# An attention and expert kernel on one core: router squares and sums reordered on ScalarE, seven masked expert inputs instead of eight, the drain's last steps in another order

## The chip, the cores and the metric

The kernel runs on one core of a Trainium2 chip. The metric is the device time of one execution in microseconds (us). Shown are three runs of the kernel before and one execution taken by the hardware profiler.

## The reference

`x` has 16 images of 256 positions and 128 channels. For each image the reference computes

```
h = layernorm(x) * (1 + ca) + sa
x = x + ga * attn(h)
h = layernorm(x) * (1 + cb) + sb
x = x + gb * ffn(h)
```

with the six modulation vectors from `silu(c) @ wmod`. `attn` computes from `h` a frequency and a phase for each position, interpolates `h` at 33 sampling points around the position, weighs them by a kernel computed from `h` (8 heads), and ends with `silu(out @ out_w.T)`. `ffn` is what the change touches:

```
logits = h @ router_w.T + router_b
_, top_k_indices = top_k(softmax(logits), 2)
mask = one_hot(top_k_indices, 8).sum(axis=-2)
out = einsum('bse,ehd,bsd->bsh', mask, expert_w, h) + einsum('bse,eh->bsh', mask, expert_b)
```

Each position has two experts, so its eight mask values sum to 2.

## The kernel before, in words

The work is cut into nine units (`UNITS`): one image, seven pairs, one image. `LAST` is unit 8, `LATE` unit 7. Each engine has its own program, written out by hand in order; semaphores tie them together. There is no scheduler: the order on an engine is the order of the calls in its loop. Loop `i` on each engine takes work of several units: the front of unit `i+1` (and its statistics of unit `i+2`), the middle of unit `i`, the back of units `i-1` and `i-2`. A call `run(i, lag, stage)` does `stage` for unit `i+lag` if there is one; `second` does it only for pairs.

- **VectorE (DVE).** The resampling matrix of an image is made in `T` by a network of six predicated copies (`network`, L802), then multiplied by the hat weights `c` into `AT`: `spread_out`, L835, four products for a pair, two for each image, each followed by `set_ends` (L845). Between the products of the two images stand small steps: `places` (L758, `eI`), `moves` (L763), `logits` (L868), `stage_masks` (L773), `best` (L874, L877), `offset` (L780, `sf`), `hits` (L884). `cells_from` (L789, `near`) follows the second pair of products. `masked` (L902) multiplies the transposed second input `h2T` by the eight expert masks, 8 x 256 elements an image. `residual` (L854) adds the attention's output, in the PSUM bank `pY`, to `x` and sums it; `total` (L907) adds the experts' output. `line` (L723 to L735) makes `nlf` from ScalarE's `th`, `product` (L813) the two small products.
- **ScalarE (ACT).** It copies and scales what TensorE leaves in PSUM: `mid_A` (L507), `mid_ao` (L515), `mid_y` (L522), `mid_gate` (L529), `back_h2T` (L540), `back_mk` (L549), `back_moe` (L556). The row statistics are its too: `sums1` (L382), `squares1` and `stats2` (L368 for the mean, L371 for the squares), `norm1` and `norm2` (L405). `front_u` (L472, L479) needs `nlf`.
- **GpSimd (POOL).** For each statistic it makes `ve` (L321), the power `rs` (L327) and `nm` (L329), first `rstd2` of unit `i-1`, then `rstd1` of unit `i+2`. `norm1` and `norm2` wait for `nm`.
- **TensorE (PE).** `mid_A` (L1051) transposes `AT`, `mid_attend` (L1065) multiplies by the values, `mid_y` (L1075) by `out_w`, `mid_gate` (L1081) transposes back into `pY`. `back_x2T` (L1091), `back_logits` (L1102) and `back_mk` (L1112) belong to the router, `back_experts` (L1136, with the bias matmul L1153) to the experts, `back_out` (L1158) transposes the experts' output back. `warm_up` (L985) are matmuls whose result nobody reads.
- **SyncE's queue.** `masks` writes the mask rows to memory and loads them back, spread over the partitions (`mkb`). The last two units get their masks by TensorE instead (`back_mb`, L1124), in four quarters of two experts.

After the loops each engine has a drain, written out call by call, in which the units `LATE-1`, `LATE` and `LAST` end. There the output of the experts of `LATE` goes to `pY`, and the statistics of `LATE` and `LAST` are VectorE's (L706 to L715).

```
                run(i, 2, sums1)
                run(i, 1, front_u)
                run(i, -1, norm2)
...
                run(i, -1, back_h2T)
                run(i, -2, back_moe)
                run(i, 2, squares1)
                run(i, 0, mid_A, 0)
```

Of the kernel before, what the change touches and what calls it, by code (L numbers as in the profile page):

```python
# [86 lines left out]
def build(nc, t):  # L87

    ctx = ExitStack()
    with ctx:  # L90
# [32 lines left out]
        sel = sb("sel", [NP * E, E, P], BF16)  # L123
# [53 lines left out]
        d_out = sem("d_out")  # L177
# [7 lines left out]
        g_nm1 = sem("g_nm1"); g_nm2 = sem("g_nm2")  # L185
# [83 lines left out]
        def _(sp):  # L269
# [19 lines left out]
            def masks(n):  # L289
# [6 lines left out]
                sp.dma_start(scratch[n % 2][:, 0:w], mkT[0:E, 0:w]).then_inc(d_mk, 16)  # L296
# [3 lines left out]
                sp.dma_start(mkb[n % 2][:, :, 0:w], spread(scratch[n % 2][:, 0:w], [P, E, w], 0)).then_inc(d_mkb[n % 2], 16)  # L300
# [55 lines left out]
        def _(act):  # L356
# [263 lines left out]
        def _(dve):  # L620
# [295 lines left out]
            for i in range(-1, LAST):  # L916
# [12 lines left out]
                run(i, 0, network, range(5, 6))  # L929
                run(i, 1, line)  # L930
# [39 lines left out]
            total(LATE - 1)  # L970
# [8 lines left out]
        def _(pe):  # L979
# [136 lines left out]
            def back_mb(n, b):  # L1116
# [23 lines left out]
            def back_biases(n, b, dst):  # L1140
                if n < LATE:
                    pe.wait_ge(v_hm, before(n) + b + 1)
                if b == 0:
# [137 lines left out]
```

## Time and profile before

| what | value |
|---|---|
| three runs | 293.69, 294.6, 295.03 us; median 294.6 |
| the profiled execution's own time | 293.6 us |
| its span, first to last instruction | 291.8 us |
| busy VectorE | 262.0 us, 90% |
| busy TensorE (matmuls) | 262.0 us, 90% |
| busy ScalarE | 226.9 us, 78% |
| busy GpSimd | 62.7 us, 21% |
| mean granted TensorE clock | 0.998 |
| ScalarE's waits for GpSimd's `nm` | 16.1 us in 10 |

The profile is of one execution. The span leaves out some 1.8 us around the instructions. "Busy" is the share in which an engine executes; a busy TensorE includes the matmuls that only keep it going. Times in the rows further down are us from the start of the span.

### The profile page before, as it was taken

What the parts mean: (1) busy time and instruction counts of PE and PEld (TensorE: products, weight loads), DVE (VectorE), ACT (ScalarE), POOL (GpSimd) and SP (SyncE); (2) the same over time, 40 slices, a digit from 0 to 9 for tenths busy, and PEclk for the clock granted to TensorE, in tenths of its full rate; (3) what the DMA queues carried; (4) which work ended last, traced back from release to release, by engine and by line L of the source; (5) the groups of instructions that cost most, each with busy time, mean ns of one, the idle gap of its engine ahead of it and who ended that gap; (6) DMA issues with size and microseconds to landing.
All of it is one profiled execution on the core that took longest, in us unless ns stands there. A gap on an engine that the chain in (4) does not pass through costs nothing.

```text
span 291.8 us, 5429 instructions
## 1 busy us (share of the span) xinstructions
PE 262.0 (90%) x1867; PEld 181.0 (62%) x1876; DVE 262.0 (90%) x543; ACT 226.9 (78%) x641; POOL 62.7 (21%) x59
## 2 busy tenths in 40 slices
PE   8899886899798999889998999889999989899995
PEld 3544642665486487647784569548884768476664
DVE  7989989998979999999999899989999999982671
ACT  4885899699897998699869989799779767655310
POOL 4103101800451023502080026202340300010100
PEclk9999999999999999999999999999999999999999
DMA  6560000020004000320014000500041004100101
GB/s 179 161 160 0 0 0 0 3 74 1 1 2 163 2 1 0 97 86 3 0 29 155 0 0 2 183 2 1 2 130 53 1 0 125 60 2 0 36 2 54
DMA packets 12011, 12.93 MB, mean 44 GB/s; under 512 B 1021, under 2 KB 10960, under 8 KB 11216
## 3 DMA queue, kind: packets, MB, share of 16 engines
q1 hardware_dynamic: 11540, 12.19, 13.9%
q10 hardware_dynamic: 444, 0.40, 0.5%
q8 instruction: 15, 0.25, 0.3%
q14 instruction: 12, 0.10, 0.1%
HBM read 10.44 MB, written 2.15 MB: 43 GB/s over the span
## 4 chain that ended last, share of the span: by engine, by line
ACT 31%; PE 26%; DVE 18%; POOL 12%; issue 11%; ACTq 0%; DVEq 0%; POOLq 0%
PE pE L1136 9%; ACT A L507 8%; DVE AT L835 8%; POOL rs L327 8%; ACT xn L405 4%; ACT c L490 4%; POOL nm L329 4%; PE pE L985 3%; ACT xn L371 3%; DVE T L802 3%; PE pY L1136 3%; PE pR L1028 2%; ACT hT L428 2%; ACT y L529 2%; DVE hm L902 2%
## 5 line engine op out<-in xcount | busy, mean ns | idle before, releaser
L802 DVE COPY_PREDICATED T<-mask,T 128x1472 f32<-128x1472 int16 (+9 forms) x54 | 76.2, 1411 | 0.5
L835 DVE TENSOR_TENSOR AT<-T,c 128x2064 f32<-128x2064 f32 x32 | 72.3, 2300 | 0.0
L1136 PE MATMUL pE<-hm,late 128*128 128x256 f32 x224 | 52.6, 386 | 0.0
L1136 PEld LDWEIGHTS pE<-hm,late 128*128 128x128 f32 x224 | 41.2, 190 | 6.6
L507 ACT ACTIVATE A<-pT 128x512 f32<-128x512 f32 x64 | 34.7, 600 | 12.6 <-PE pT L1051 12.5
L327 POOL TENSOR_TENSOR rs<-ve,mhalf 128x4 f32<-128x4 f32 (+1 forms) x18 | 32.5, 1806 | 44.3 <-DVE ve L715 37.5
L321 POOL TENSOR_SCALAR ve<-sq 128x4 f32<-128x4 f32 (+1 forms) x14 | 7.0, 502 | 162.9 <-ACT xn L371 162.9
L405 ACT ACTIVATE xn<-x,nm,rs 128x128 f32<-128x128 f32 x64 | 26.5, 485 | 16.1 <-POOL nm L329 16.1
L1051 PE MATMUL pT<-first,AT 128*128 128x128 f32 x256 | 34.2, 276 | 4.8 <-DVE AT L845 4.7
L1051 PEld LDWEIGHTS pT<-first,AT 128*128 128x128 f32 x256 | 28.3, 141 | 11.4 <-DVE AT L845 9.9
L507 ACT ACTIVATE A<-pR 128x512 f32<-128x512 f32 x64 | 35.2, 619 | 0.0
L1065 PE MATMUL pY<-A,hs 128*32 128x256 f32 x512 | 33.3, 384 | 1.7 <-ACT A L507 1.4
L1051 PE MATMUL pR<-first,AT 128*128 128x128 f32 x256 | 33.6, 274 | 0.0
L902 DVE TENSOR_TENSOR hm<-mkb,h2T 128x2048 f32<-128x2048 bf16 x13 | 29.6, 2276 | 0.0
L1051 PEld LDWEIGHTS pR<-first,AT 128*128 128x128 f32 x256 | 28.7, 141 | 0.6
L490 ACT ACTIVATE c<-near,early 128x172 f32<-128x172 f32 (+1 forms) x54 | 26.2, 571 | 0.0
L1028 PE MATMUL pR<-proj,hT 128*128 128x297 f32 x62 | 23.8, 465 | 0.9 <-ACT hT L428 0.9
L1065 PEld LDWEIGHTS pY<-A,hs 128*32 128x32 f32 x512 | 16.7, 109 | 12.1 <-ACT A L507 7.4
L985 PE MATMUL pE<-warm 128*128 128x512 bf16 x85 | 22.1, 415 | 1.3 <-DVE warm L643 1.2
L329 POOL TENSOR_TENSOR nm<-mu,rs 128x4 f32<-128x4 f32 (+1 forms) x18 | 21.0, 1165 | 1.4
L371 ACT ACTIVATE xn<-x,mu 128x128 f32<-128x128 f32 x52 | 20.2, 390 | 0.5
L985 PEld LDWEIGHTS pE<-warm 128*128 128x128 bf16 x88 | 9.2, 107 | 12.0 <-issue 2.8
(145 smaller groups left out, 389.2 us busy)
## 6 DMA issues: line engine op xcount, KB each, us to landing
mkb<-mask_rows SPq DMA_DIRECT2D x6, 1024.0 KB, 5.3
x<-in_x SPq DMA_DIRECT2D x7, 256.0 KB, 6.1
out<-x SPq DMA_DIRECT2D x7, 256.0 KB, 5.3
late<-in_late SPq DMA_DIRECT2D x1, 592.0 KB, 3.9
mkb<-mask_rows SPq DMA_DIRECT2D x1, 512.0 KB, 3.6
x<-in_x SPq DMA_DIRECT2D x2, 128.0 KB, 3.7
wmod<-in_wmod ACTq DMA_DIRECT2D x1, 256.0 KB, 3.5
out<-x SPq DMA_DIRECT2D x2, 128.0 KB, 3.2
```

The source lines that it names most:

```text
L327: nc.gpsimd.tensor_tensor(rs[:, 0:w], ve[:, 0:w], mhalf[:, 0:w], ALU.pow).then_inc(out, 1)
L329: nc.gpsimd.tensor_tensor(nm[:, 0:w], mu[:, 0:w], rs[:, 0:w], ALU.mult).then_inc(last, 1)
L405: ins = nc.scalar.activation(xn[:, bt, :], of_x(n)[:, bt, :], ACT.Identity, bias=nm[:, bt:bt + 1], scale=rs[:, bt:bt + 1])
L490: nc.scalar.activation(cells[:, :, :, r], near[:, 0:w, :], ACT.Abs, bias=off[:, r:r + 1]).then_inc(a_abs, 1)
L507: nc.scalar.activation(A[b][:, m, 2 * j:2 * j + 2, :].rearrange("p h l -> p (h l)"), four_banks(k)[:, :], ACT.Copy).then_inc(a_A, 1)
L802: nc.vector.copy_predicated(rows[:, :, :, j0:j1], spread(mask[:, k, 0:w, j0:j1], [P, w, H, j1 - j0], 2), rows[:, :, :, j0 + (1 << bit):j1 ...
L835: nc.vector.tensor_tensor(cells_of(bt).rearrange("p h (j r) -> p h j r", r=BLK), spread(T[n % 2][:, bt, 0:H, 0:NB], [P, H, NB, BLK], 3), s ...
L902: nc.vector.tensor_tensor(hm[b][:, :, :], mkb[n % 2][:, :, b * L:(b + 1) * L], spread(own, [P, E, L], 1), ALU.mult).then_inc(v_hm, 1)
L985: mm(bank[:, :], warm[:, 0:P], warm[:, :], start=True, stop=True)
L1051: ins = nc.tensor.transpose(four_banks(k)[:, c0:c0 + P], AT[:, 2 * b + i, 2 * j + a, OVER + m * P:OVER + (m + 1) * P], ident)
L1065: ins = mm(pY[32 * j:32 * j + 32, b * L:(b + 1) * L], hs[n % 2][:, 2 * b + m, hh, :], A[b][:, m, hh, :], start=(m == 0 and a == 0), stop=( ...
L1136: ins = mm(dst, weT[:, e, :], hm[b][:, e, :], start=False, stop=(e == E - 1))
```

## The change

The change has three parts.

1. *Experts.* Since the eight mask values of a position sum to 2, the sum over eight masked experts is written as `2 W7 h` plus the sum over seven of `mask_e (W_e - W7) h`. `expert_weights` makes the differences and the doubled `W7` once, in loop 1 (`selectors` moves from loop 0's end to behind its network). `masked` then makes seven inputs, the mask transfers and `back_mb` carry seven, and `back_plain` multiplies `h2T` by `2 W7`, 512 columns for a pair, with one bias matmul for both images.
2. *Order in the loops.* On ScalarE `sums1` goes behind `norm2`, and `squares1` ahead of `back_moe`. On TensorE the last two experts of a pair go behind `back_x2T`, and four warm-ups of each loop from 3 on go. In loop `LATE` the masks of unit `LATE-1` are made between the two halves of `mid_A`, and their transfer is issued by image.
3. *The drain.* On VectorE both masked products of `LATE-1`, `residual(LATE)` and `stats2(LATE)` come ahead of the last `AT` product, which also waits for `rs2`. ScalarE and TensorE follow that order.

```diff
             def masks(n):
...
-                sp.dma_start(scratch[n % 2][:, 0:w], mkT[0:E, 0:w]).then_inc(d_mk, 16)
+                sp.dma_start(scratch[n % 2][:, 0:w], mkT[0:EM, 0:w]).then_inc(d_mk, 16)
...
+                parts = ((0, L, d_mkb[n % 2]), (L, w, d_mkl)) if n == LATE - 1 else ((0, w, d_mkb[n % 2]),)
+                for c0, c1, landed in parts:
+                    sp.dma_start(mkb[n % 2][:, :, c0:c1],
+                                 spread(scratch[n % 2][:, c0:c1], [P, EM, c1 - c0], 0)).then_inc(landed, 16)
...
# ScalarE, loop
-                run(i, 2, sums1)
                 run(i, 1, front_u)
                 run(i, -1, norm2)
                 if i < 0:
                     run(i, 1, front_hs)
+                run(i, 2, sums1)
                 run(i, -1, back_h2T)
+                run(i, 2, squares1)
                 run(i, -2, back_moe)
-                run(i, 2, squares1)
-                run(i, 0, mid_A, 0)
-                run(i, -1, back_mk)
+                run(i, 0, mid_A, 0, (0,))
+                if i == LATE:
+                    back_mk(LATE - 1)
+                run(i, 0, mid_A, 0, (1,))
+                if i < LATE:
+                    run(i, -1, back_mk)
                 run(i, 2, norm1)
...
# ScalarE, drain
             mid_gate(LATE)
+            back_moe(LATE - 1)
+            norm2(LATE)
+            back_h2T(LATE)
             mid_A(LAST, 0)
-            norm2(LATE)
+            back_mk(LATE)
             mid_ao(LAST)
-            back_h2T(LATE)
             mid_y(LAST)
             mid_gate(LAST)
-            back_mk(LATE)
-            back_moe(LATE - 1)
             norm2(LAST)
...
# VectorE
+            def expert_weights():
+                dve.wait_ge(d_late, 32)
+                nc.vector.tensor_tensor(weT[:, 0:EM, :], weT[:, 0:EM, :], spread(weT[:, EM, :], [P, EM, C], 1),
+                                        ALU.subtract).then_inc(v_we, 1)
+                dve.wait_ge(v_we, 1)
+                nc.vector.tensor_scalar(weT[:, EM, :], weT[:, EM, :], 2.0, None, ALU.mult).then_inc(v_we, 1)
...
                 run(i, 0, network, range(5, 6))
+                if i == 0:
+                    selectors()
+                elif i == 1:
+                    expert_weights()
                 run(i, 1, line)
...
-            network(LAST, range(2, 6))
+            network(LAST, range(2, 3))
             masked(LATE - 1, 0)
+            network(LAST, range(3, 5))
+            masked(LATE - 1, 1)
+            network(LAST, range(5, 6))
+            residual(LATE)
+            stats2(LATE)
+            dve.wait_ge(g_rs2, LATE + 1)
             spread_out(LAST, 0)
             spread_out(LAST, 1)
             set_ends(LAST, 0)
-            masked(LATE - 1, 1)
-            residual(LATE)
-            stats2(LATE)
             route(LATE)
             residual(LAST)
             stats2(LAST)
+            total(LATE - 1)
             masked(LATE, 0)
-            total(LATE - 1)
...
# TensorE
+            def back_plain(n):
...
+                w = tiles(n) * P
+                mm(moe_bank(n)[:, 0:w], weT[:, EM, :], h2T_of(n)[:, 0:w], start=True, stop=False)
+                mm(moe_bank(n)[:, 0:w], ebp[:, :], mkT_of(n)[:, 0:w], start=False, stop=False)
...
                 run(i, -2, back_experts, 0)
-                second(i, -2, back_experts, 1)
+                second(i, -2, back_experts, 1, range(0, 5))
                 if i == 1:
-                    warm_up(18)
+                    warm_up(23)
...
                 run(i, -1, back_x2T)
-                if i > 0:
+                second(i, -2, back_experts, 1, range(5, EM))
+                if 0 < i < 3:
                     warm_up(4, pT[0])
...
+            back_experts(LATE - 1, 0, range(0, 4))
             mid_y(LATE)
-            back_experts(LATE - 1, 0)
+            back_experts(LATE - 1, 0, range(4, EM))
             mid_gate(LATE)
+            back_experts(LATE - 1, 1)
+            warm_up(6, pT[0])
+            back_x2T(LATE)
+            back_out(LATE - 1)
+            back_logits(LATE)
+            warm_up(4, pT[0])
             mid_A(LAST, 0, 0)
             mid_A(LAST, 0, 1)
+            back_mk(LATE)
             mid_attend(LAST, 0, 0)
             mid_attend(LAST, 0, 1)
...
```

How the instructions stand now, at the three places that matter. ScalarE, in a steady loop, from the squares of the second statistic to the first copy of `A`. Before:

```order
L368 ACTIVATE mu2<-sum2 128x4
L371 ACTIVATE xn2,sq2<-x,mu2 128x128 x4
L452 ACTIVATE hs1<-pX 128x16x2x16
L382 ACTIVATE xn1,sum1<-x 128x128 x4
L472 ACTIVATE u<-early,nlf,invf 128x50 x4
L479 ACTIVATE uR<-u 128x200
L405 ACTIVATE xn2<-x,nm2,rs2 128x128 x4
L540 ACTIVATE h2T<-pX,modT 128x256 x2
L556 ACTIVATE moeT<-pE,modT 128x256 x2
L368 ACTIVATE mu1<-sum1 128x4
L371 ACTIVATE xn1,sq1<-x,mu1 128x128 x4
L507 ACTIVATE A0<-pT0 128x512
```

Now:

```order
L373 ACTIVATE mu2<-sum2 128x4
L376 ACTIVATE xn2,sq2<-x,mu2 128x128 x4
L457 ACTIVATE hs1<-pX 128x16x2x16
L477 ACTIVATE u<-early,nlf,invf 128x50 x4
L484 ACTIVATE uR<-u 128x200
L410 ACTIVATE xn2<-x,nm2,rs2 128x128 x4
L387 ACTIVATE xn1,sum1<-x 128x128 x4
L545 ACTIVATE h2T<-pX,modT 128x256 x2
L373 ACTIVATE mu1<-sum1 128x4
L376 ACTIVATE xn1,sq1<-x,mu1 128x128 x4
L561 ACTIVATE moeT<-pE,modT 128x256 x2
L512 ACTIVATE A0<-pT0 128x512
```

The sums (`xn1,sum1`) moved behind `norm2` (`xn2<-x,nm2,rs2`), the router squares (`mu1`, `xn1,sq1`) ahead of `moeT`.

VectorE, in the drain, from the last network's third stage on; `T0` is the matrix of `LAST`, `hm0` and `hm1` are the masked inputs of the two images of `LATE-1`. Before:

```order
L802 COPY_PREDICATED T0<-mask,T0 128x2x8x46 x2
L802 COPY_PREDICATED T0<-mask,T0 128x2x8x44
L802 COPY_PREDICATED T0<-mask,T0 128x2x8x43
L902 TENSOR_TENSOR hm0<-mkb0,h2T 128x2048
L835 TENSOR_TENSOR AT<-T0,c 128x8x258 x2
L845 COPY AT<-endw 128x16x2
L902 TENSOR_TENSOR hm1<-mkb0,h2T 128x2048
L854 SCALAR_TENSOR_TENSOR x,sum2<-pY,x 128x128 x4
L706 BN_STATS st2<-x 128x6 x4
L710 BN_AGGR mv2<-st2 128x2 x4
L714 TENSOR_SCALAR mu2<-mv2 128x4
L715 TENSOR_SCALAR ve2<-mv2 128x4
```

Now:

```order
L923 TENSOR_TENSOR hm1<-mkb0,h2T 128x1792
L820 COPY_PREDICATED T0<-mask,T0 128x2x8x43
L872 SCALAR_TENSOR_TENSOR x,sum2<-pY,x 128x128 x4
L724 BN_STATS st2<-x 128x6 x4
L728 BN_AGGR mv2<-st2 128x2 x4
L732 TENSOR_SCALAR mu2<-mv2 128x4
L733 TENSOR_SCALAR ve2<-mv2 128x4
L853 TENSOR_TENSOR AT<-T0,c 128x8x258 x2
L863 COPY AT<-endw 128x16x2
L886 TENSOR_TENSOR lg<-pL,rb 128x32
```

The last `AT` product moved from ahead of the second masked product to behind the statistics of `LATE`.

TensorE, in the drain, around `mid_y(LATE)` (L1075, `pY<-aoT`). Before:

```order
L1065 MATMUL pY<-A1,hs1 32x256 x16
L1075 MATMUL pY<-aoT,late 128x512
L1153 MATMUL pE<-mkT,ebp 128x256
L1136 MATMUL pE<-hm0,late 128x256 x8
L1081 MATMUL pY<-first,y 128x128 x4
```

Now:

```order
L1094 MATMUL pY<-A1,hs1 32x256 x16
L1185 MATMUL pE<-h2T,late 128x512
L1186 MATMUL pE<-mkT,ebp 128x512
L1167 MATMUL pE<-hm0,late 128x256 x4
L1104 MATMUL pY<-aoT,late 128x512
L1167 MATMUL pE<-hm0,late 128x256 x3
L1110 MATMUL pY<-first,y 128x128 x4
L1167 MATMUL pE<-hm1,late 128x256 x7
L1014 MATMUL pT0<-warm 128x512 x6
L1120 MATMUL pX<-first,xn2 128x128 x4
```

The plain matmul (`pE<-h2T`), the bias and four experts of `LATE-1` moved ahead of `mid_y`.

## Rows read from the trace of the kernel before

**Rows 1.** Busy time by stretch: length; PE, PEld, DVE, ACT, POOL busy; clock; DMA

```profile
127.55:159.33 31.78, 29.18 (x218) 21.01 (x218) 30.46 (x57) 28.17 (x84) 8.48 (x6) 1.00 0.15 43
```

**Rows 2.** Timeline of VectorE, 140 to 174 (start us, length us, engine, line, operation)

```profile
139.29 4.52 DVE L835 TENSOR_TENSOR AT<-T,c 128x2064 f32<-128x2064 f32 x2
...
146.02 0.32 DVE L780 SCALAR_TENSOR_TENSOR sf<-sc,u 128x172 f32<-128x172 f32 x1
...
146.53 4.52 DVE L835 TENSOR_TENSOR AT<-T,c 128x2064 f32<-128x2064 f32 x2
...
163.44 0.29 DVE L854 SCALAR_TENSOR_TENSOR x<-pY,x 128x128 f32<-128x128 f32 x1 [0.99 <-PE pY L1081]
...
168.82 0.16 DVE L734 SCALAR_TENSOR_TENSOR nlf<-lp,invf 128x4 f32<-128x4 f32 x1
...
171.06 4.52 DVE L835 TENSOR_TENSOR AT<-T,c 128x2064 f32<-128x2064 f32 x2
```

**Rows 3.** Timeline of ScalarE (ACT), 140 to 174

```profile
142.23 1.02 ACT L540 ACTIVATE h2T<-pX,modT 128x256 f32<-128x256 f32 x2 [0.75 <-PE pX L1091]
...
143.85 0.21 ACT L368 ACTIVATE mu<-sum 128x4 f32<-128x4 f32 x1
...
152.59 1.65 ACT L405 ACTIVATE xn<-x,nm,rs 128x128 f32<-128x128 f32 x4 [2.54 <-POOL nm L329]
...
166.52 0.19 ACT L368 ACTIVATE mu<-sum 128x4 f32<-128x4 f32 x1
...
168.77 0.29 ACT L382 ACTIVATE xn<-x 128x128 f32<-128x128 f32 x1
...
169.94 1.37 ACT L472 ACTIVATE u<-early,nlf,invf 128x50 f32<-128x50 f32 x4
...
171.62 1.63 ACT L405 ACTIVATE xn<-x,nm,rs 128x128 f32<-128x128 f32 x4
```

**Rows 4.** Timeline of GpSimd (POOL), 140 to 174

```profile
146.19 6.00 POOL L327 TENSOR_TENSOR rs<-ve,mhalf 128x4 f32<-128x4 f32 x1
...
170.03 0.77 POOL L329 TENSOR_TENSOR nm<-mu,rs 128x4 f32<-128x4 f32 x1
```

**Rows 5.** Timeline of GpSimd, round 2

```profile
83.36 1.01 POOL L327 TENSOR_TENSOR rs<-ve,mhalf 128x4 f32<-128x4 f32 x1
...
84.44 4.47 POOL L329 TENSOR_TENSOR nm<-mu,rs 128x4 f32<-128x4 f32 x1
```

**Rows 6.** Groups by line and form, the masked product

```profile
L902 DVE TENSOR_TENSOR hm<-mkb,h2T 128x2048 f32<-128x2048 bf16 x13 | 29.6, 2276 | 0.0
```

**Rows 7.** Timeline of TensorE (PE), 140 to 174

```profile
160.00 1.12 PE L1075 MATMUL pY<-aoT,late 128*128 128x512 f32 x2
...
165.83 3.72 PE L1136 MATMUL pE<-hm,late 128*128 128x256 f32 x16
```

**Rows 8.** Timeline of VectorE, rounds 1 and 2

```profile
43.52 0.22 DVE L723 TENSOR_REDUCE sums<-th 128x8 f32<-128x64 f32 x1 [0.96 <-ACT th L463]
...
81.93 0.19 DVE L868 TENSOR_TENSOR lg<-pL,rb 128x32 f32<-128x32 f32 x1 [1.92 <-PE pL L1102]
```

**Rows 9.** Timeline of TensorE, the drain

```profile
250.91 1.12 PE L1075 MATMUL pY<-aoT,late 128*128 128x512 f32 x2 [0.94 <-ACT aoT L515]
...
260.70 2.26 PE L1065 MATMUL pY<-A,hs 128*32 128x256 f32 x32
...
272.46 0.28 PE L1153 MATMUL pY<-mkT,ebp 24*128 24x256 bf16 x1
```

**Rows 10.** Timeline of VectorE, the drain

```profile
256.81 0.20 DVE L845 COPY AT<-endw 128x32 f32<-128x32 f32 x1
...
259.10 0.29 DVE L854 SCALAR_TENSOR_TENSOR x<-pY,x 128x128 f32<-128x128 f32 x1
...
269.17 0.28 DVE L854 SCALAR_TENSOR_TENSOR x<-pY,x 128x128 f32<-128x128 f32 x1
```

**Rows 11.** Timeline of GpSimd, the drain

```profile
261.77 1.01 POOL L327 TENSOR_TENSOR rs<-ve,mhalf 128x4 f32<-128x4 f32 x1 [29.68 <-DVE ve L715]
```

More of the change, by code:

```diff
@@ L20 @@
 E = 8
+EM = E - 1
 EPS = 1e-5
@@ L159, in build @@
         mkT = sb("mkT", [NP * E, BT * P], BF16); mkL = sb("mkL", [NP * E, L], BF16)
-        mkb = [sb(f"mkb{i}", [P, E, BT * P], BF16) for i in range(2)]
-        hm = [sb(f"hm{i}", [P, E, L]) for i in range(2)]
+        mkb = [sb(f"mkb{i}", [P, EM, BT * P], BF16) for i in range(2)]
+        hm = [sb(f"hm{i}", [P, EM, L]) for i in range(2)]
         moeT = sb("moeT", [P, BT * P])
-        scratch = nc.dram_tensor("mask_rows", (2, E, BT * P), BF16, kind="Internal").ap()
+        scratch = nc.dram_tensor("mask_rows", (2, EM, BT * P), BF16, kind="Internal").ap()
         pT = [bank("pT0"), bank("pT1")]
@@ L901, in masked @@
                     dve.wait_ge(d_mkb[n % 2], 16 * (n // 2 + 1))
+                elif n == LATE - 1:
+                    dve.wait_ge(d_mkl, 16)
                 nc.vector.tensor_tensor(hm[b][:, :, :], mkb[n % 2][:, :, b * L:(b + 1) * L],
-                                        spread(own, [P, E, L], 1), ALU.mult).then_inc(v_hm, 1)
+                                        spread(own, [P, EM, L], 1), ALU.mult).then_inc(v_hm, 1)
             def total(n):
@@ L1122, in back_mb @@
                         pe.wait_ge(v_hm, masked_before(before(n) + b - 1) + k + 1)
-                    for a in range(2):
+                    for a in range(min(2, EM - 2 * k)):
                         ins = mm(four_banks(k)[:, a * L:(a + 1) * L], sel[:, 2 * k + a, :], mkT_of(n)[:, b * L:(b + 1) * L],
@@ L1126, in back_mb, with back_experts @@
                     ins.then_inc(t_mb, 1)
-            def back_experts(n, b, own=range(E)):
+            def back_experts(n, b, own=range(EM)):
                 img = before(n) + b
-                dst = moe_bank(n)[:, b * L:(b + 1) * L]
                 if own[0] == 0:
-                    back_biases(n, b, dst)
+                    if b == 0:
+                        back_plain(n)
+                    if n < LATE:
+                        pe.wait_ge(v_hm, img + 1)
                 for e in own:
@@ L1135, in back_experts @@
                         pe.wait_ge(v_hm, masked_before(img) + e // 2 + 1)
-                    ins = mm(dst, weT[:, e, :], hm[b][:, e, :], start=False, stop=(e == E - 1))
-                if own[-1] == E - 1:
+                    ins = mm(moe_bank(n)[:, b * L:(b + 1) * L], weT[:, e, :], hm[b][:, e, :], start=False,
+                             stop=(e == EM - 1 and b == UNITS[n][1] - 1))
+                if own[-1] == EM - 1:
                     ins.then_inc(t_moe, 1)
[L1140 to L1143, printed above, removed]
-                    pe.wait_ge(a_mk, n + 1)
-                    if n == 0:
-                        pe.wait_ge(v_ebp, 8)
-                    if n == LATE:
-                        pe.wait_ge(v_x2, NU)
-                    elif n == LAST:
-                        pe.wait_ge(v_out, LATE)
-                    elif n > 0:
-                        pe.wait_ge(v_out, n)
-                mm(dst, ebp[:, :], mkT_of(n)[:, b * L:(b + 1) * L], start=True, stop=False)
+            def back_plain(n):
+                if n == 0:
+                    pe.wait_ge(v_ebp, 8)
+                    pe.wait_ge(v_we, 2)
+                if n == LATE:
+                    pe.wait_ge(v_x2, NU)
+                elif n == LAST:
+                    pe.wait_ge(v_out, LATE)
+                elif n > 0:
+                    pe.wait_ge(v_out, n)
+                pe.wait_ge(a_mk, n + 1)
+                w = tiles(n) * P
+                mm(moe_bank(n)[:, 0:w], weT[:, EM, :], h2T_of(n)[:, 0:w], start=True, stop=False)
+                mm(moe_bank(n)[:, 0:w], ebp[:, :], mkT_of(n)[:, 0:w], start=False, stop=False)
             def back_out(n):
@@ L1194, in _ @@
                 run(i, -2, back_out)
+                if i == LATE:
+                    back_mk(LATE - 1)
                 run(i, 0, mid_A, 0, 1)
-                run(i, -1, back_mk)
+                if i < LATE:
+                    run(i, -1, back_mk)
                 run(i, 0, mid_attend, 0, 0)
@@ L1224, in _ @@
             back_mb(LATE, 1)
-            back_experts(LATE, 0, range(6, E))
+            back_experts(LATE, 0, range(6, EM))
             back_experts(LATE, 1, range(0, 3))
@@ L1229, in _ @@
             back_mb(LAST, 0)
-            back_experts(LATE, 1, range(6, E))
+            back_experts(LATE, 1, range(6, EM))
             back_experts(LAST, 0, range(0, 4))
             back_out(LATE)
-            back_experts(LAST, 0, range(4, E))
+            back_experts(LAST, 0, range(4, EM))
             back_out(LAST)
```

26 lines of the change are left out of this document (9 added, 17 removed).

## The prediction

> **What bounds the kernel now.** I read the busy shares of a steady round first. A round is the work between the first `AT` product of one unit and that of the next; round i is the one of loop i. VectorE is busy 30.46 of 31.78 us, TensorE 29.18, ScalarE 28.17, at a granted clock of 1.00 [rows 1]. The product starts at 139.29 and again at 171.06, so a round takes 31.77. VectorE idles once worth mention: 0.99 us ahead of `residual`, for `pY` from TensorE [rows 2]. Behind that wait stands ScalarE's order: its one long wait is 2.54 us ahead of `norm1` (152.59), for GpSimd's `nm1` [rows 3]. GpSimd is late because its power (`rs`) takes 6.00 us there against 1.01 elsewhere [rows 4, 5]. The long one began at 146.19, inside VectorE's `sf` (146.02), and ended only after the next `AT` pair (146.53) and `near` [rows 2]. In round 2 `rs` began at 83.36, clear of `sf`, took 1.01, and then `nm` was the one held, 4.47 [rows 5]. So a GpSimd instruction that begins before `sf` passes, and one that begins in it waits out the pair.
>
> **Masked inputs: seven for eight.** A product of 2048 elements takes 2276 ns [rows 6]; 256 fewer at the same rate save 0.28, and with a fixed part 0.27. Two per round: 0.54 us of VectorE. TensorE loses two f32 matmuls of 256 columns, 3.72 for eight or 0.465 each, and gets one of 512, which the one of the same size in `mid_y` puts at 1.12 at most [rows 7]. The two bias matmuls become one. I count TensorE as even there, and lighter by the four warm-ups that go from each steady round; both are worth nothing while its 2.6 us of idle cover them (with that gone, at most the 0.2 by which 1.12 exceeds two experts). The mask transfers shrink by an eighth, and nobody waits for them. `selectors` moves into VectorE's wait for `th` at the end of loop 0, `expert_weights` (896 and 128 elements at the rate of rows 6, 1.2 us, an estimate) into the one at the end of loop 1, which is 0.96 long [rows 8] and grows by the 0.6 that `selectors` leaves. Both cost nothing; without that cover they would cost 1.8 once.
>
> **ScalarE's order in a round.** I walk one round from its first product (0), in the times of rows 2 and 3, with a length T. Before: squares of `x2` start at 27.23, sums at 29.48, `u` at 30.65, `norm2` at 32.33, `h2T` at 2.94 of the next round, the router squares behind `moeT` from 4.56. The power then begins at 6.9, inside `sf` (6.73). Now `u` follows `hs` at once, but needs `nlf`, written 2.1 before the next product. So `u` starts at T-1.95 and `norm2` at T-0.15, when `nm2` has come. It takes 1.55, and the sums (29.48 to 30.65, 1.17) fill the time in which TensorE transposes, so `h2T` starts at 2.6. It takes 0.9 and the squares 1.8 (2.25 from 27.23 to the sums, less `hs`); with `moeT` behind them they end at 5.3. With `ve` ahead, which the mask product may hold to 5.9, the power starts at 6.1, before `sf`: it passes. `nm1` is held till `near` is through, some 1.0 before the 6.00 ended at 152.19, so it comes at about 12.1 and `norm1` starts at 12.2, not 13.30. From `norm1` to `residual` it was 10.85 (163.44 less 152.59). So `residual` may start at 23.05, where VectorE, 0.27 shorter by then, is ready at 22.85. VectorE's wait falls from 0.99 to 0.2. T is then 31.77 - 0.54 - 0.8 = **30.4**, and VectorE is the bound. What is next late is `pY` again, by 0.2; then the logits, which come 2.05 after `h2T` starts, at 4.65, and are needed at 5.1 (both estimates). TensorE's 29.2 at most fit in 30.4.
>
> The Trainium skill (SBUF — State Buffer, Who interferes with whom) says that a VectorE instruction with two SBUF inputs and a GpSimd instruction that reads SBUF exclude each other, the first to issue holding the port for its whole instruction. By that rule as it stands `rs` would have got in between `sf` and the next product; the 6.00 speaks against so early a release. By the rule `norm1` would wait less and T would be 0.2 shorter, some 0.7 over the steady rounds.
>
> Rounds: the first product of round 3 comes 0.9 earlier (three shorter masked products, 0.8, and the logits of round 2). Three steady rounds give 1.37 each, 4.1. The round of the last pair had no wait: 0.55. **Together -5.6 us** at the start of the drain. Bounds: masks alone (0.27 to 0.5 a round) 2.3, and 7.5 with all of VectorE's idle gone.
>
> **The drain.** Times here are those of before; the 5.6 comes off all. TensorE is free of the last pair's attention at 249.97 (250.91 less its wait of 0.94) [rows 9]. It then does the plain and bias matmuls and four experts, 1.4 + 1.86, ahead of `mid_y`, which moves to 253.2. From `mid_y` to `residual` a round takes 3.44 [rows 2, 7], so `residual(LATE)` starts at 256.65, against 259.10 [rows 10]: 2.45 earlier, with VectorE idle in front, since both masked products and the network are done by 253.9 (256.81 less the product pair, 4.5, less 0.27, plus 1.9 for the second masked product). But the last `AT` product now waits for `rs2`. From `residual` to the end of that power it took 3.68 [rows 10, 11], so the product starts at 260.4 and, with its 4.5 and the `COPY`, ends at 265.1. Before, the `COPY` ended at 257.0. From the `COPY`'s start to the end of attention it was 6.15 (262.96) [rows 9, 10]; the mask matmuls `back_mk` now lie between, 0.6. Attention ends at 271.8. Copy, `mid_y`, silu, gate and transpose of one image follow with nothing beside them, 2.4 as an estimate (the 3.44 is for two images and with other work between). `residual(LAST)` starts at 274.2, against 269.17. The first matmuls of `LATE`'s experts write `pY` too and wait for it: 274.8, against 272.46 [rows 9]. That is 2.3 later. Behind them the order is as before; one expert and one mask matmul fewer per image are used up by the plain matmul and by a masked quarter that comes 0.7 behind it. I take **+2.5 us** for the drain. Bounds: 0, if my walk misses an overlap (the filled 6 us of VectorE), and +7 below.
>
> **Sum.** 293.6 (own time of the profiled execution, span 291.8) - 5.6 + 2.5 = 290.5. The median shown, 294.6, lies 1.0 above that execution; I carry half of it: **291.0 us**. A measurement here tells about 0.5%, 1.5 us, from no change.
>
> **Rivals.**
> 1. *`nm2` of the last pair is held.* VectorE's wait is for `rs2`, not `nm2`. Both engines wake on the same event. If the product takes the port first, `nm2` waits for one product, 2.2; that it can get in between two VectorE instructions shows at 170.03, held by the small product there and through after 0.77 [rows 4]. `norm2`, `h2T`, the logits and, behind them on TensorE, the transposes of `A(LAST)` all come 2.2 later: 293.2, with the half added as in the sum. Against it: VectorE has further waits to pass before the product, while `nm2` needs 0.2. The skill's same section says that issue order decides; by it the tie is open too. If held over both products, as at 84.44 [rows 5], it is 4.4, 295.4.
> 2. *The power stays stuck.* The squares end 1.1 earlier than before, of which 0.6 is margin to `sf`. If `u` or `h2T` come later than I walk, `norm1` stays at 13.3, T is 31.5, and the rounds give only masks, 2.3: 294.3, no change.
> 3. *`norm2` becomes the late one: slower.* It now stands directly ahead of the sums, and nothing covers its wait. `nm2` ran from 170.03 to 170.80, 0.26 before the product at 171.06 [rows 2, 4]. Once it begins after the product does, it waits for the product's end, 2.2. `norm2`, the sums and `h2T` follow, and VectorE waits for the logits, as round 2 shows with 1.92 [rows 8]. If this held in five rounds, T would be 30.4 + 2 = 32.4, 0.6 longer than now: 293.6 + 3 + 2.5 + 0.5, 299.6. It decides where `nm2` starts behind the product, that is where the squares of `x2` (29.0 at their end before, 1.75 ahead of `nm2`) end later than T-1.75. I have T-2.5, a margin of 0.75; before it was 1.0.
> 4. *The drain costs nothing:* 288.5, if `back_mk` and the warm-ups hide and the experts run on.
>
> **Chances.** Forecast 0.5, rival 1 0.15, rival 2 0.15, rival 3 0.1, rival 4 0.1. Faster by over 0.5% (below 293.1): forecast, rival 4 and half of rival 1, 0.67. Within 0.5%: rival 2 and part of rival 1, 0.2. Slower: 0.13. The range 287.5 to 295.0 takes in all but rival 3 and tails.
>
> **What would show it.** Product to product 30.4 in steady rounds, `residual`'s wait 0.2 or less, `rs` near 1 and `nm` above 4 in them, `norm1` waiting about 1.8. `hm` products near 2.0 us. In the drain VectorE idles about 2.7 ahead of `residual(LATE)` and 7 to 8 ahead of `residual(LAST)`, and from the last `COPY` of the loops to the end it takes 2.5 longer. It is wrong if rounds stay at 31.5, if `lg` waits in every round, or if `nm2` of the last pair takes over 2 us.

## The result

| what | before | changed |
|---|---|---|
| runs | 294.81 us median (293.69 to 295.07, 4 runs) | **298.58 us** median (297.81 to 301.05, 4 runs) |
| profiled execution: own time, span | 293.6, 291.8 | 298.4, 296.6 |
| mean granted clock of TensorE | 0.998 | 0.983 |
| start of `LATE`'s second `AT` product | 239.23 | 233.72 |
| from there to the end of the last `total`, "the tail" below | 50.33 | 60.65 |

The changed kernel is slower: ratio 1.015, 95% interval 1.0085 to 1.0214. The forecast was 291.0, with 287.5 to 295.0 as its range; the time lies outside, on the other side of no change. The last two rows of the table split it: the loops give back 5.51 us, the drain takes 10.32 more. Executions over 1.5% above the fastest of their kernel count in the medians and ranges below but not in the ratios: one each of `e2`, `e7` and `e9`, and one of the kernel before beside `e1` to `e4` and one beside `e5` to `e8`.

From the page of the changed kernel: the busy shares, the granted clock in 40 slices (7.4 us each), and one group of instructions.

```profile
PE 263.5 (89%) x1847; PEld 179.1 (60%) x1847; DVE 258.7 (87%) x545; ACT 228.2 (77%) x641; POOL 53.6 (18%) x59
...
PEclk9999999999999999999999999999999999959799
...
L923 DVE TENSOR_TENSOR hm<-mkb,h2T 128x1792 f32<-128x1792 bf16 x13 | 26.2, 2015 | 0.0
```

The masked product takes 2015 ns against 2276 [rows 6]. The clock row has two dents near the end.

**A steady round, as forecast.** Busy time of the same round as [rows 1], with its columns:

```profile
137.40:167.68 30.28, 28.08 (x213) 20.04 (x212) 29.90 (x58) 28.29 (x83) 8.19 (x6) 1.00 0.14 41
```

VectorE in it; these answer to [rows 2]:

```profile
137.40 4.52 DVE L853 TENSOR_TENSOR AT<-T,c 128x2064 f32<-128x2064 f32 x2
...
143.98 0.31 DVE L798 SCALAR_TENSOR_TENSOR sf<-sc,u 128x172 f32<-128x172 f32 x1
...
160.29 0.29 DVE L872 SCALAR_TENSOR_TENSOR x<-pY,x 128x128 f32<-128x128 f32 x1
...
167.68 4.51 DVE L853 TENSOR_TENSOR AT<-T,c 128x2064 f32<-128x2064 f32 x2
```

GpSimd, answering to [rows 4, 5]:

```profile
143.36 1.01 POOL L332 TENSOR_TENSOR rs<-ve,mhalf 128x4 f32<-128x4 f32 x1
144.44 4.88 POOL L334 TENSOR_TENSOR nm<-mu,rs 128x4 f32<-128x4 f32 x1
```

And ScalarE, answering to [rows 3]:

```profile
139.89 0.99 ACT L545 ACTIVATE h2T<-pX,modT 128x256 f32<-128x256 f32 x2
...
149.44 1.65 ACT L410 ACTIVATE xn<-x,nm,rs 128x128 f32<-128x128 f32 x4 [1.65 <-POOL nm L334]
...
165.64 1.39 ACT L477 ACTIVATE u<-early,nlf,invf 128x50 f32<-128x50 f32 x4
...
167.45 1.65 ACT L410 ACTIVATE xn<-x,nm,rs 128x128 f32<-128x128 f32 x4
```

The power begins 0.62 ahead of `sf` and takes 1.01, `nm` is held instead, `norm1` starts 12.04 into the round, `residual` has no wait, and the round takes 30.28.

**The drain.** VectorE, answering to [rows 10]:

```profile
251.18 0.29 DVE L872 SCALAR_TENSOR_TENSOR x<-pY,x 128x128 f32<-128x128 f32 x1 [3.04 <-PE pY L1110]
...
254.89 4.53 DVE L853 TENSOR_TENSOR AT<-T,c 128x2064 f32<-128x2064 f32 x2 [1.19 <-POOL rs L332]
...
262.73 0.19 DVE L886 TENSOR_TENSOR lg<-pL,rb 128x32 f32<-128x32 f32 x1 [3.08 <-PE pL L1131]
...
274.45 0.29 DVE L872 SCALAR_TENSOR_TENSOR x<-pY,x 128x128 f32<-128x128 f32 x1 [10.19 <-PE pY L1110]
...
293.95 0.42 DVE L928 TENSOR_TENSOR x<-pE,x 128x256 f32<-128x256 f32 x1 [1.67 <-PE pE L1191]
```

GpSimd, answering to [rows 11]:

```profile
253.85 1.01 POOL L332 TENSOR_TENSOR rs<-ve,mhalf 128x4 f32<-128x4 f32 x1 [27.27 <-DVE ve L733]
254.93 2.32 POOL L334 TENSOR_TENSOR nm<-mu,rs 128x4 f32<-128x4 f32 x1
```

The product began 0.04 ahead of `nm2` and held it over one product: 2.32 in place of 0.2. The prediction had named an `nm2` of over 2 us as a sign of being wrong. TensorE, answering to [rows 9]:

```profile
254.00 1.46 PE L1014 MATMUL pT<-warm 128*128 128x512 bf16 x6
...
259.05 0.66 PE L1120 MATMUL pX<-first,xn 128*128 128x128 f32 x4 [3.59 <-ACT xn L410]
260.82 1.88 PE L1131 MATMUL pL<-late,h2T 128*128 128x8 f32 x8 [0.67 <-ACT h2T L545]
...
264.21 1.91 PE L1080 MATMUL pT<-first,AT 128*128 128x128 f32 x8
...
275.02 1.12 PE L1185 MATMUL pY<-h2T,late 128*128 128x512 f32 x2 [0.60 <-DVE x L872]
...
277.29 3.39 PE L1167 MATMUL pY<-hm,late 128*128 128x256 f32 x8 [0.82 <-DVE hm L915]
```

TensorE idles 3.59 us for `norm2`, 2.1 of them because `nm2` is held (with `nm2` free, in `e2`, it idles 1.48), and what follows runs at about half speed. The busy time by stretch (columns as in [rows 1]) has the clock:

```profile
256.00:258.00 2.00, 0.00 (x0) 0.00 (x0) 2.00 (x2) 0.65 (x2) 1.25 (x1) 1.00 0.00 0
...
260.00:262.00 2.00, 1.33 (x8) 1.19 (x6) 0.00 (x0) 0.76 (x2) 0.00 (x0) 0.66 0.00 0
262.00:264.00 2.00, 2.00 (x8) 1.17 (x8) 1.20 (x14) 0.00 (x0) 0.00 (x0) 0.50 0.00 0
...
278.00:280.00 2.00, 2.00 (x6) 1.59 (x5) 0.75 (x2) 0.12 (x1) 0.00 (x0) 0.50 0.27 72
```

0.50 is the lower of the clock's two levels, 1.2 GHz against 2.4. In the 2 us from 256 TensorE does nothing, and the clock is at 0.50 from 262 to 266 and again from 278 to 280. These are two falls; only the first has a long idle of TensorE ahead of it. The Trainium skill (TensorE: Matmul & The Clock Gate, "What's actually happening") says that the clock follows how busy TensorE has recently been and is throttled by default. The trace agrees with the first half of that: the first fall comes behind the stretch without work.

### The profile page after: what moved, and what is told of

Read it like the earlier page. It is cut to its first block, busy times and chain, and to the rows that moved or that the text cites. A ratio compares the mean times of both kernels' runs of the same rounds, so it can differ in the third digit from the quotient of the medians.

```text
span 296.6 us, 5391 instructions
## 1 busy us (share of the span) xinstructions
PE 263.5 (89%) x1847; PEld 179.1 (60%) x1847; DVE 258.7 (87%) x545; ACT 228.2 (77%) x641; POOL 53.6 (18%) x59
## 4 chain that ended last, share of the span: by engine, by line
ACT 33%; DVE 27%; PE 18%; POOL 11%; issue 10%; ACTq 0%; DVEq 0%; POOLq 0%
DVE AT L853 8%; POOL nm L334 8%; ACT A L512 8%; DVE T L820 5%; ACT xn L410 5%; ACT xn L376 4%; PE pY L1167 3%; ACT c L495 3%; PE pT L1080 3%; ACT y L534 2%; POOL rs L332 2%; ACT hT L433 2%; PE pE L1167 2%; PE pR L1080 2%; PE pY L1094 2%
## 5 line engine op out<-in xcount | busy, mean ns | idle before, releaser
L1167 PE MATMUL pE<-hm,late 128*128 128x256 f32 x196 | 45.8, 383 | 0.0
L1080 PE MATMUL pT<-first,AT 128*128 128x128 f32 x256 | 35.1, 281 | 6.3 <-DVE AT L863 6.3
L1167 PEld LDWEIGHTS pE<-hm,late 128*128 128x128 f32 x196 | 36.0, 190 | 6.3 <-issue 1.8
L326 POOL TENSOR_SCALAR ve<-sq 128x4 f32<-128x4 f32 (+1 forms) x14 | 5.7, 407 | 168.6 <-ACT xn L376 168.6
L1080 PE MATMUL pR<-first,AT 128*128 128x128 f32 x256 | 34.3, 278 | 0.0
L1080 PEld LDWEIGHTS pR<-first,AT 128*128 128x128 f32 x256 | 29.5, 144 | 0.5
L334 POOL TENSOR_TENSOR nm<-mu,rs 128x4 f32<-128x4 f32 (+1 forms) x18 | 28.3, 1570 | 1.4
L332 POOL TENSOR_TENSOR rs<-ve,mhalf 128x4 f32<-128x4 f32 (+1 forms) x18 | 17.5, 973 | 53.0 <-DVE ve L733 46.2
L923 DVE TENSOR_TENSOR hm<-mkb,h2T 128x1792 f32<-128x1792 bf16 x13 | 26.2, 2015 | 0.0
L872 DVE SCALAR_TENSOR_TENSOR x<-pY,x 128x128 f32<-128x128 f32 x32 | 7.5, 291 | 14.7 <-PE pY L1110 14.3
```

Source lines behind the costliest of these rows:

```text
L334: nc.gpsimd.tensor_tensor(nm[:, 0:w], mu[:, 0:w], rs[:, 0:w], ALU.mult).then_inc(last, 1)
L1080: ins = nc.tensor.transpose(four_banks(k)[:, c0:c0 + P], AT[:, 2 * b + i, 2 * j + a, OVER + m * P:OVER + (m + 1) * P], ident)
L1167: ins = mm(moe_bank(n)[:, b * L:(b + 1) * L], weT[:, e, :], hm[b][:, e, :], start=False, stop=(e == EM - 1 and b == UNITS[n][1] - 1))
```

## The experiments

Each was timed beside the kernel before, whose median on the same chips was 293.34 (`e1` to `e4`), 293.55 (`e5` to `e8`) and 293.35 (`e9`).

**e1_old_drain.** The changed loops with the drain of before, brought to seven experts. Of the three engines' calls, a piece of ScalarE's and one of VectorE's:

```
-            norm2(LATE)
-            back_h2T(LATE)
             mid_A(LAST, 0)
-            back_mk(LATE)
+            norm2(LATE)
...
-            residual(LATE)
-            stats2(LATE)
-            dve.wait_ge(g_rs2, LATE + 1)
             spread_out(LAST, 0)
             spread_out(LAST, 1)
             set_ends(LAST, 0)
+            masked(LATE - 1, 1)
+            residual(LATE)
+            stats2(LATE)
             route(LATE)
```

> The change with the drain of before on VectorE, ScalarE and TensorE (seven inputs and the loops' new order stay). Theory (the loops gained 5.5 us, the new drain lost 10.3): 294.8 - 5.5, about 289.0 us, ratio 0.98, clock 1.00 up to the last 4 us. Rival A (the loops' gain is only a shift that the drain gives back through another wait): 293 to 295. Rival B (the order of the loops suits only the new drain): above 296.

Measured: 288.19 us (287.91 to 288.54, 4 runs), ratio 0.9816 (0.978 to 0.9852), clock 1.00. VectorE in its drain:

```profile
233.81 4.52 DVE L853 TENSOR_TENSOR AT<-T,c 128x2064 f32<-128x2064 f32 x2
...
246.61 4.53 DVE L853 TENSOR_TENSOR AT<-T,c 128x2064 f32<-128x2064 f32 x2
...
282.41 0.42 DVE L928 TENSOR_TENSOR x<-pE,x 128x256 f32<-128x256 f32 x1 [1.67 <-PE pE L1187]
```

The loops keep their gain; the tail is 49.02, 1.3 shorter than before (fewer experts) and 11.6 shorter than in the changed kernel. So the whole loss lies in the drain's order. Between the two profiled executions the span fell by 6.7 but the time by 5.7: what lies around the span is 2.8 here and 1.8 before, which no run explains.

**e2_wait_nm.** VectorE waits for `nm2` instead of `rs2`.

```
-            dve.wait_ge(g_rs2, LATE + 1)
+            dve.wait_ge(g_nm2, LATE + 1)
```

> The change, with VectorE's wait ahead of the last AT product for nm2 instead of rs2. Theory (the product took the port 0.04 us before nm2 began and held it for 2.3; norm2, logits and behind them the transposes of A(LAST) came late): nm takes 0.2, norm2 starts 2 us earlier, the time falls by 2 to 4.5, to 294 to 296.5. Rival (the 2.3 lie beside the product itself, which the transposes wait for anyway): no change, 298.5.

Measured: 296.38 (292.93 to 297.39, 9 runs), ratio 1.0058 (1.0017 to 1.0098). GpSimd, and below it VectorE:

```profile
257.39 0.20 POOL L334 TENSOR_TENSOR nm<-mu,rs 128x4 f32<-128x4 f32 x1
```

```profile
257.62 4.53 DVE L853 TENSOR_TENSOR AT<-T,c 128x2064 f32<-128x2064 f32 x2 [1.47 <-POOL nm L334]
...
271.58 0.29 DVE L872 SCALAR_TENSOR_TENSOR x<-pY,x 128x128 f32<-128x128 f32 x1 [7.78 <-PE pY L1110]
```

TensorE, and its clock further on:

```profile
259.39 0.66 PE L1120 MATMUL pX<-first,xn 128*128 128x128 f32 x4 [1.48 <-ACT xn L410]
```

```profile
274.00:276.00 2.00, 1.59 (x4) 1.32 (x5) 1.88 (x4) 0.88 (x2) 0.20 (x2) 0.50 0.45 131
```

For 0.28 more of waiting `nm2` takes 0.20, and `residual(LAST)` comes 13.96 behind the product, not 19.56. It is then 35.42 behind `LATE`'s product, where the changed kernel has 40.73: this one edit takes away the held `nm2` (2.1) and, as TensorE now idles 1.48 and the clock stays at 1.00 there, the first fall as well (3.2). The clock falls once later (0.50 from 274 to 280), behind `residual(LAST)`, and in this execution also once in the first loops. The tail is 56.71. The Trainium skill (SBUF — State Buffer, "Who interferes with whom") says of this pair of engines that whoever issues first keeps the port for its whole instruction: in the drain of the changed kernel, with 0.04 us between them, the trace agrees, and putting `nm2` first undid it. In its steady round it does not: there `nm` is the one recorded 0.04 ahead (144.44 against 144.48) and is held for 4.88 all the same. So a start some hundredths earlier in a trace doesn't tell which engine holds the port.

**e3_warm.** 22 warm-up matmuls where the changed kernel has 6; `nm2` still held.

```
-            warm_up(6, pT[0])
+            warm_up(22, pT[0])
             back_x2T(LATE)
```

> The change with 22 warm-ups instead of 6 ahead of the transposes of x2(LATE) in the drain, so TensorE has no idle 3.6 us. Theory (that idle time brought the granted clock to 0.5 for 7 us, in which logits, warm-ups and the first 16 transposes took double): the clock stays at 1.00 from 254 to 270, the transposes of A(LAST) end 3.3 earlier, time 295 to 295.5. A second fall near 277 may stay. Rival (the clock falls whatever fills the gap, or the work waits for something else): 298 to 299.

Measured: 295.17 (293.59 to 297.26, 10 runs), ratio 1.0051 (1.0019 to 1.0083); the profiled execution took 293.81 at clock 1.00, span 292.0. GpSimd, then TensorE:

```profile
255.18 2.32 POOL L334 TENSOR_TENSOR nm<-mu,rs 128x4 f32<-128x4 f32 x1
```

```profile
254.46 4.70 PE L1014 MATMUL pT<-warm 128*128 128x512 bf16 x21
259.30 0.66 PE L1120 MATMUL pX<-first,xn 128*128 128x128 f32 x4
261.06 1.06 PE L1131 MATMUL pL<-late,h2T 128*128 128x8 f32 x8 [0.67 <-ACT h2T L545]
...
262.83 1.04 PE L1080 MATMUL pT<-first,AT 128*128 128x128 f32 x8
...
272.04 1.13 PE L1185 MATMUL pY<-h2T,late 128*128 128x512 f32 x2 [0.60 <-DVE x L872]
```

This is the price of both falls, read from one execution of each kernel. The transposes of `xn` start as late as in the changed kernel (25.34 behind `LATE`'s product, 25.33 there), nothing else is moved, and the tail is 55.82: **4.8 us less**. 3.2 of it lie ahead of `residual(LAST)`, where the first fall was, and 1.6 behind, where the second was. These warm-ups fill the idle of the first; why the second stayed away in this execution isn't shown. Four of the ten executions had the clock at 1.000 and took 293.59 to 293.87; the other six, at 0.981 to 0.994, took 294.97 to 297.26. So the clock still fell somewhere in six of ten; where is not on record.

**e4_drain_only.** The kernel before, with all eight inputs and its loops, and the new drain with the masks by the image.

```
+            network(LAST, range(5, 6))
+            residual(LATE)
+            stats2(LATE)
+            dve.wait_ge(g_rs2, LATE + 1)
             spread_out(LAST, 0)
             spread_out(LAST, 1)
```

> The kernel before with the new drain alone (eight inputs, loops as before, masks of LATE-1 early and by image). Theory (the drain alone costs what the change lost, 10.3 less the eighth input's share): 302 to 306 us, clock falling in the drain as in the change. Rival (the drain is only bad behind the faster loops): under 298. My first walk, with the order's cost alone and neither the held nm nor the clock: 297.

Measured: 305.68 (304.75 to 305.99, 4 runs), ratio 1.0397 (1.0354 to 1.0441), clock 0.966. GpSimd and VectorE:

```profile
260.55 2.32 POOL L332 TENSOR_TENSOR nm<-mu,rs 128x4 f32<-128x4 f32 x1
```

```profile
260.50 4.53 DVE L842 TENSOR_TENSOR AT<-T,c 128x2064 f32<-128x2064 f32 x2 [1.18 <-POOL rs L330]
```

The tail is 61.40: the same held `nm2`, the same two falls of the clock (TensorE idles 2.76 ahead of the first), and one more in the first loops. The drain costs its full price (11 us of tail) without the changed loops, and e1 shows the loops' gain without the drain.

**e5_nm_warm.** The wait of e2 and 12 warm-ups.

```
-            dve.wait_ge(g_rs2, LATE + 1)
+            dve.wait_ge(g_nm2, LATE + 1)
...
-            warm_up(6, pT[0])
+            warm_up(12, pT[0])
```

> The change, waiting for nm2 instead of rs2 and with 12 warm-ups instead of 6 ahead of the transposes of x2(LATE). Theory (held nm and clock are two separate costs; what is left is the new order's own): from the second product of LATE to the end 53.5 to 54.5 us in the trace, against 60.7 in the change, 56.7 with nm alone and 55.8 with 22 warm-ups alone; clock 1.00; time about 293 in executions without an early fall. Rival (the two costs overlap, one cure takes both): 55.5 to 56.5.

Measured: 293.45 (292.81 to 294.51, 10 runs), ratio 0.999 (0.9967 to 1.0013): no change against before. `residual(LAST)` starts 13.95 behind the product, where I had 13.8. The tail is 54.40, inside the theory's range, but its condition failed: the clock fell in the first loops and again behind `residual(LAST)` (0.50 from 272 to 274). Nor does the run show two separate costs. `residual(LAST)` is 35.40 behind `LATE`'s product, as with `nm2` alone (35.42 in e2), so the warm-ups added nothing up to there; the 2.3 by which this tail is shorter than e2's lie behind it, in a shorter second fall. That the tail met the forecast is luck in that part.

**e6_act_old.** e1 with ScalarE's loop order of before, so that of the loops' changes only seven inputs and TensorE's order remain.

```
+                run(i, 2, sums1)
                 run(i, 1, front_u)
                 run(i, -1, norm2)
...
-                run(i, 2, sums1)
                 run(i, -1, back_h2T)
-                run(i, 2, squares1)
                 run(i, -2, back_moe)
+                run(i, 2, squares1)
```

> The run with the drain of before, and in ScalarE's loop also the order of before (sums ahead of u, squares behind moeT), so that seven inputs and TensorE's order stay. Theory (the round is set by norm1 waiting for a power that is stuck behind the AT pair): rs takes 6 in the rounds again, norm1 waits 2 to 3, T is 31.4 to 31.6, time 291 to 292. Rival (seven inputs gave the whole gain): T 30.25, time 288.2.

Measured: 287.95 (287.12 to 288.41, 4 runs), ratio 0.9803 (0.9779 to 0.9828): as fast as e1. A steady round takes 30.06. VectorE and GpSimd:

```profile
144.80 0.32 DVE L798 SCALAR_TENSOR_TENSOR sf<-sc,u 128x172 f32<-128x172 f32 x1
145.31 4.51 DVE L853 TENSOR_TENSOR AT<-T,c 128x2064 f32<-128x2064 f32 x2
```

```profile
144.98 1.01 POOL L332 TENSOR_TENSOR rs<-ve,mhalf 128x4 f32<-128x4 f32 x1
146.06 1.60 POOL L334 TENSOR_TENSOR nm<-mu,rs 128x4 f32<-128x4 f32 x1
```

This refutes my rule for the power. Here `rs` begins 0.18 inside `sf`; before it began 0.17 inside and took 6.00 [rows 2, 4]; here it takes 1.01, and `nm` gets in between the two products. ScalarE's new order isn't needed for the loops' gain; the rival holds. No run parts the seven inputs from TensorE's new order.

**e7_act_only.** The kernel before with ScalarE's new order alone (the edit of e6 reversed).

> The kernel before with ScalarE's new order in the loops alone, eight inputs, drain of before. Theory: rs takes 1.0 in the rounds, residual's wait falls from 0.99 to under 0.3, T is 30.8 to 31.0, time 290.5 to 291.5. Rival (the new order needs the shorter masked products): T stays 31.8, time 293 to 294.

Measured: 290.44 (289.38 to 304.14, 9 runs), ratio 0.9883 (0.9849 to 0.9918). GpSimd:

```profile
143.53 1.01 POOL L327 TENSOR_TENSOR rs<-ve,mhalf 128x4 f32<-128x4 f32 x1
144.62 4.84 POOL L329 TENSOR_TENSOR nm<-mu,rs 128x4 f32<-128x4 f32 x1
```

The order alone does free the power, as I had walked it: a round takes 30.52 to 30.57. So each part frees it by itself, and the two gains overlap: 1.2 a round by ScalarE's order, 1.7 by seven inputs with TensorE's order, 1.5 by all of it.

**e8_y_first.** e5 with `mid_y(LATE)` ahead of the experts of `LATE-1`, the remaining ones behind the gate, 6 warm-ups.

```
-            back_experts(LATE - 1, 0, range(0, 4))
             mid_y(LATE)
-            back_experts(LATE - 1, 0, range(4, EM))
+            back_experts(LATE - 1, 0, range(0, 2))
             mid_gate(LATE)
+            back_experts(LATE - 1, 0, range(2, EM))
```

> The run with nm2 and warm-ups, and in the drain mid_y(LATE) ahead of the experts of LATE-1 (two experts between it and mid_gate, six warm-ups instead of twelve). Theory (the four experts and the plain matmul ahead of mid_y hold residual(LATE), and the last AT product with it): residual's wait in the drain falls from 3.0 to about 0.6, the product and the end come 2 to 2.4 earlier, 51.5 to 52 from LATE's second product to the end, time about 291. Rival (the wait is beside TensorE's own work, which then comes later): no change against the run with nm2 and warm-ups.

Measured: 294.61 (293.01 to 297.03, 10 runs), ratio 1.0053 (1.0024 to 1.0083). VectorE:

```profile
253.40 4.53 DVE L853 TENSOR_TENSOR AT<-T,c 128x2064 f32<-128x2064 f32 x2 [1.46 <-POOL nm L334]
...
269.26 0.29 DVE L872 SCALAR_TENSOR_TENSOR x<-pY,x 128x128 f32<-128x128 f32 x1 [7.79 <-PE pY L1110]
```

The product starts 19.76 behind `LATE`'s, against 21.45 in e5, but `residual(LAST)` comes 15.86 behind it instead of 13.95. TensorE only owes its experts later: the rival holds. The tail is 55.34; the clock fell behind `residual(LAST)` here too.

**e9_nm_warm18.** The wait of e2 and 18 warm-ups.

> The wait for nm2 in place of rs2, and 18 warm-up matmuls (not 6) ahead of the last pair's transposes: both things that the forecast of the drain left out are taken away, and what is left is the moved order by itself. From the start of LATE's second AT product to the start of the last total the kernel before takes 50.33 us, the changed one 60.65. Theory A (the order costs the forecast 2.5, the held nm2 about 2, and the rest of the 10.3 is TensorE at half clock): granted clock 1.00 through the drain, nm 0.20, AT(LAST) some 21.5 behind LATE's product, residual(LAST) waits 7.8, this stretch 50.33 + 2.5 + 0.3 (the new wait) = 53.1 to 53.6; median 291.5 to 293.0. Theory B (the order itself costs 5 or more, since behind the plain matmul the experts are late as well): the stretch stays at 55 or above with the clock at 1.00 throughout, median 294 or more.

Measured: 295.03 (292.41 to 296.83, 10 runs), ratio 1.0032 (1.0004 to 1.006). The condition of both theories, a clock of 1.00, held in one execution of ten. The profiled one (296.76, clock 0.975) has a fall in the first loops and one behind `residual(LAST)`:

```profile
PEclk9999959999999999999999999999999999999599
```

The one execution at clock 1.000 took 292.41, span 290.6; those at 0.994 took 293.39 to 294.26, those at 0.975 took 296.8. The first speaks for theory A, one execution only. (What both theories call the stretch to the start of the last `total` runs to its end.) The profiled stretch is 57.49, with the fall in it. The 18 warm-ups have a price of their own: `residual(LAST)` is 14.85 behind the product, 0.9 more than in e5.

## Why the prediction was wrong, step by step

| step | forecast | measured |
|---|---|---|
| masked product shorter by | 0.27 | 0.26 |
| round | 30.4 | 30.28 |
| power, `nm1`, `norm1` in the round | 1, over 4, at 12.2 | 1.01, 4.88, at 12.04 |
| start of the drain | -5.6 | -5.51 |
| `residual(LATE)` (less 5.6) | 251.05 | 251.18 |
| last `AT` product | 254.8 | 254.89 |
| `COPY` behind it ends | 259.5 | 259.65 |
| `residual(LAST)` | 268.6 | **274.45** |
| plain matmul | 269.2 | **275.02** |
| tail against before | +2.5 | **+10.32** |

**Right:** the loops, and the drain up to the last product, each start within 0.16 us. The loops' cause was right in the changed kernel, but not the only way there: e6 gets the same gain without ScalarE's order, where the forecast had put 0.54 a round on the masks and 0.8 on that order. And the rule that a GpSimd instruction which begins in `sf` waits out the pair fell.

**Wrong:** the step from the last product to `residual(LAST)`, VectorE's wait of 7 to 8 there, which measured 10.19 behind a further 3.08 for the logits. Two things sit in it.

1. *Rival 1 came true.* I gave it 0.15 on the ground that VectorE has further waits to pass while `nm2` needs only 0.2. It has none that last: the product was first by 0.04 in the changed kernel, and by 0.05 in e3 and e4. My price, 2.2 for one product, was right for the instruction (2.32 less 0.20), but not for what hangs on it: releasing `nm2` alone, in e2, brings `residual(LAST)` 5.3 forward, 3.2 of that by the clock. (The range was said to take in all but rival 3; this rival's second form, 295.4, lay outside it too.) Rival 1 gave 293.2; e3, where `nm2` is held and the clock stays up, took 293.81 in its profiled execution.
2. *TensorE's clock was in no term of the sum.* That is the step that failed. I gave VectorE's waits of 2.7 and 7 to 8, and never walked TensorE through the same stretch. There `nm2`, `norm2` and the transposes follow one another with nothing to run but six warm-ups. The idle grew to 3.59 and the clock fell behind it: 3.2. A second fall, behind `residual(LAST)`, cost 1.6 more. It has no long idle ahead of it and came in all profiled executions of the new drain but e3's, at 0.7 (e5) to 3.0 (e2), and once behind the old drain (e7). e3, without either fall, prices the two at 4.8 us, the difference between no change and slower.

**The order's own cost.** Put together from e5, up to the plain matmul (270.42 less 234.46 is 35.96, against 33.23 before, less 0.28 for the new wait) it is 2.45, forecast 2.3. Behind it, from e3 (17.74 against 17.10), it is 0.64, forecast 0.2. Together 3.1 where I had 2.5. The held `nm2` costs 2.4: the plain matmul starts 38.08 behind `LATE`'s product in e3 and 35.96 in e5, and e5 pays 0.28 for its wait. Then 3.1 + 2.4 + 4.8 (clock) = 10.3, what was measured. But the kernel before isn't the drain to compare with: with seven inputs the old drain is 1.3 shorter than before, so against e1 the new order costs 4.4 even at full clock and with `nm2` free.

`residual(LATE)` 2.4 earlier bought nothing, as the last image's product, on which the rest hangs, was put behind it: 246.61 in e1, 254.89 in the changed kernel.

The best version is the one of e6 or e1: 288.0 to 288.2 us, ratio 0.980 to 0.982 of before, the loops' changes with the drain left as it was.

**Open:** why `rs` was held before and not in e6, with 0.01 us between their places in `sf`; what makes the clock fall in the first loops in some executions (the profiles of e2, e4, e5 and e9 show it, the others don't); what makes it fall behind `residual(LAST)`; and how large the drain's cost is with the clock at 1.00 and `nm2` free, of which no profile was taken. Put together it is 3.4, with the 0.28 of the wait, and with e9's 0.9 for its warm-ups this gives a span of 291.8 - 5.5 + 3.4 + 0.9 = 290.6, which is what e9's one execution at clock 1.000 had.

## What to carry to other kernels

Where a change puts a new chain of small steps between two stretches of TensorE's work, walk TensorE through it too: behind an idle of some 3.6 us the work here ran at half clock and came 3.2 later, more than the 2.1 of the held instruction that had made the idle so long. Where VectorE and GpSimd are released by the same event, wait for the last of GpSimd's small instructions; 0.28 us of waiting stood against 2.1 and the 3.2 behind it. And when a change has parts in the loops and in the drain, time them apart: here one part gave 5.5 us and the other took 10.3.

## What the runs showed of the hardware beyond what was expected

- A GpSimd instruction of 0.20 us took 2.32 behind one `AT` product, 4.88 behind a pair, and 1.60 where it came in the first product of a pair and was through about where that ended. That it passes between the two products in some cases (changed kernel's drain, e3, e4, e6) and not in others (steady rounds of the changed kernel and of e7) has no cause in these traces.
- The same work at the lower clock: eight transposes of `AT` 1.91 against 1.04, eight experts 3.39 against 1.99 (part of them at full clock), eight matmuls for the logits 1.88 against 1.06.
- A fall can come without the long idle: in e9 TensorE was busy 1.35 to 1.48 of each 2 us from 268 to 274, and the clock went to 0.50 behind it. These are the stretches:

```profile
268.00:270.00 2.00, 1.48 (x19) 0.64 (x12) 0.00 (x0) 0.39 (x2) 0.00 (x0) 1.00 0.00 0
270.00:272.00 2.00, 1.35 (x10) 0.75 (x9) 0.47 (x4) 0.89 (x2) 0.00 (x0) 1.00 0.00 0
272.00:274.00 2.00, 1.44 (x3) 0.39 (x3) 1.90 (x10) 0.00 (x0) 0.69 (x1) 0.89 0.00 0
274.00:276.00 2.00, 1.64 (x4) 1.37 (x5) 1.83 (x4) 0.88 (x2) 0.19 (x1) 0.50 0.45 131
```

- In e3 the same matmuls ran in the same order through this place, and the clock stayed at 1.00 in the profiled execution. In e3's other executions the mean clock ranged from 0.981 to 1.000, so the same program runs with and without falls; where they were isn't on record.
